# A Mamba-and-attention kernel on one core: output products of high and low parts, B's table re-read through DRAM, divisions one per tile

## The chip, the core and the metric

The kernel runs on one core of a Trainium2 chip. Its five engines are TensorE (PE; its weight loads are shown as PEld), VectorE (DVE), ScalarE (ACT), GpSimd (POOL) and SyncE (SP, which here only issues DMAs). The metric is device time in microseconds (us) of one execution, lower is better.

## The reference, cut to what matters

The reference is a block of a state-space layer (L0) and an attention layer (L1), both residual, on x of shape (4, 1024, 512). The change is in L0's scan and in L1's last projection. What L0 computes, cut:

```python
xr, gate = jnp.split(x @ W_in.T, 2, axis=-1)
xc = silu(conv(xr + t_emb))                      # 4 taps, per channel
xn = layernorm(xc) * ln_g + ln_b                 # (4, 1024, 1024)
Bm, Cm, dt = jnp.split(xn @ W_xproj.T, 3, axis=-1)
Ad = 1.0 + tanh(dt @ W_dt.T + b_dt) * 0.01 * A
def step(h, inputs):                             # 1024 steps, h is (4, 16, 1024)
    h = jnp.clip(h * ad[:, :, None] + bd[:, :, None] * xt[:, None, :], -10.0, 10.0)
    return h, jnp.einsum('bd,bdh->bh', ct, h)
y = ys + D * xn
x1 = x + (y * silu(gate)) @ W_out.T
```

L1 is attention with 16 heads; at its end the attended rows are divided by the softmax sums and multiplied with w_weight.

## The kernel before, in words

The kernel goes through a pre-phase (in-projection, convolution, norm; up to about 435 us), the scan (466 to 1422 us), a short phase in which the scan's last tiles are put out beside the first work of L1 (1427 to 1491 us), the projections of L1, the attention, and an out phase (2799 us to the end).

**The scan.** `scan_phase` has 32 iterations (`LOOPS`) of 32 steps, and each iteration has 16 pairs of steps (`PAIRS`). All four batches go through each step together. VectorE does the recurrence, one custom instruction of 128x512 a step (L905). Each engine has its own program, ordered by hand, and they meet on semaphores. In `pe_loop` TensorE's order for two pairs v and v+1 is: the outer products of B and x for pair v (`products_bx`, L1023, into the PSUM tile `bx`, one of two buffers); in some places a `turn`, four transposes of the gated rows `yg` into `p_turn`; two pieces from `ORDER`; the outer products for pair v+1; the readouts of pairs v-2 and v-1 (L1033). I call such two pairs a period. There are eight in an iteration, and `ORDER` gives them: gate, gate, out, out, gate, gate, out, out. A gate piece is three fp32r products of 128x128 by 128x512 (high by high, high by low, low by high; L940). An out piece is one of the eight products (m = 0 to 7) of the output projection of tile j, one plain fp32 matmul, which the profile shows as two instructions (L949). The turns stand in the periods v = 0 (a gate period) and v = 4 (an out period). For the first five iterations (`OUT_LAG`) there is no tile to put out, and each out piece is replaced by four fp32r products whose result nobody reads (L955).

**What stands around an out piece.** A tile of 128 rows is mixed by POOL (`mix`, L910, L913, L916: times D, plus the scan's y, times the gate, into `yg`), turned by TensorE, copied by ACT from `p_turn` to `yg_t` (`take_turned`, L973), multiplied, and copied out by ACT (`take_out`, L977). ACT takes the first half's turn right after the last four stores of the scan's y of the iteration before (L1079).

**B's table.** POOL writes `b_weights` and `c_weights` for each half (i = 0 and 1) of an iteration (L1007, L1009) as soon as the buffer is free, and TensorE waits for them at the first pair of that half. `b_weights` comes from `bd_all`, a table of B of 128 partitions by 16 KB. It is spread from DRAM by `load_bd`: twelve DMAs, whose source has a leading dimension of 4 or 2 copies with step 0. The part for the first four iterations is loaded ahead of the scan, under `consts_in`, for which VectorE waits before its last two set-up instructions; the rest is loaded inside the scan, under `bd_in`, for which POOL waits only ahead of iteration 4. SP issues the loads of x (`load_moving`, eight DMAs a half) as the buffers come free.

**After the scan** five tiles are still to be put out (`out_tile`); VectorE does their mixes, and POOL scales x1 for L1 (`scale_x1`, L195).

**The out phase.** For each of 32 tiles TensorE multiplies into one of four PSUM banks, and VectorE scales (L1831) and adds the residual (L1823). The last batch's four row blocks are first divided by the softmax sums on VectorE (`divide`, L1750), cast by ACT (L1809) and their low parts are taken by POOL (L1817). Tile 24 is the first that needs them.

Of the kernel before, what the change touches and what calls it, by code (L numbers as in the profile page):

```python
# [8 lines left out]
f32 = mybir.dt.float32  # L9
f32r = mybir.dt.float32r  # L10
# [4 lines left out]
P = 128  # L15
# [728 lines left out]
def scan_phase(nc, I, Xp, Xn, Bp, Pd, Iv, Cm, Y, SG, X1, pj, shared, used_before):  # L744
# [26 lines left out]
    with ExitStack() as ctx:  # L771
# [6 lines left out]
        w_out = sb("w_out", [P, NM, MODEL], f32); d_row = sb("d_row", [P, INNER], f32); ident = sb("ident", [P, P], f32)  # L778
        y = sb("y", [P, INNER], f32)
        w_plain = shared; xn, sg_in, yg = (shared[:, i, :] for i in range(3)); yg_t = shared[:, 3, :].rearrange("p (m t) -> p m t", t=P)  # L780
# [5 lines left out]
        bd_all = sb("bd_all", [P, SEQ // PHASES * STATES], f32)  # L786
# [17 lines left out]
        w_high = sem("w_high"); x_high = sem("x_high"); x_split = sem("x_split"); others_in = sem("others_in"); xn_in = sem("xn_in"); y_in = sem("y_in"); res_in = sem("res_in"); mixed = sem("mixed"); gated = sem("gated"); turned = sem("turned"); turned_taken = sem("turned_taken")  # L804
        out_ready = sem("out_ready"); out_taken = sem("out_taken"); x1_ready = sem("x1_ready"); x1_out = pj.x1_out
        consts_in = sem("consts_in"); bd_in = sem("bd_in"); zeros_ready = sem("zeros_ready")
# [10 lines left out]
        EARLY = LAG * (STEPS // PHASES) * STATES  # L817

        def load_bd(e, done, begin, end, phases):
            for phase in phases:  # L820
                for row, part, copies in ((0, 0, 4), (4, 1, 2), (6, 0, 2)):
                    src = Bp[part, :, phase].rearrange("(o b) t d -> o b (t d)", o=1)[:, :, begin:end].to_broadcast([copies, BATCH, end - begin])
                    e.dma_start(bd_all[phase * GROUP + row * BATCH:phase * GROUP + (row + copies) * BATCH, begin:end], src).then_inc(done, 16)
# [8 lines left out]
        with nc.Block() as block:  # L832
            @block.sync
            def _(sp):
# [7 lines left out]
                load_bd(sp, consts_in, 0, EARLY, range(2, PHASES))  # L842
# [3 lines left out]
            def _(act):  # L846
                load_moving(act, 0, 0)
                act.dma_start(x_tile[:], I["x_tiles"][0]).then_inc(tile_in, 16)
                load_bd(act, consts_in, 0, EARLY, range(2))
# [57 lines left out]
        def mix(e, engine, j):  # L907

            e.wait_ge(xn_in, START + j * 32 + 32)
            engine.tensor_tensor(out=xn, in0=xn, in1=d_row[:], op=ALU.mult).then_inc(mixed, 1)  # L910
# [20 lines left out]
        def piece_of(pe, it, j, piece):  # L931
# [66 lines left out]
        def pool_loop(pool, it, j, out=False, split=True):  # L998
            for i in range(2):
                if i == 1 and split:  # L1000
                    split_low(pool, it)
# [913 lines left out]
```

## Time and profile before

| | |
|---|---|
| time, median of 3 runs | 2910.11 us (2899.70 to 2910.88) |
| the profiled execution | 2906.17 us, span 2904.4 us |
| mean granted TensorE clock | 0.968 of 2.4 GHz |
| PE busy | 2739.1 us, 94% of the span |
| DVE busy | 2006.8 us, 69% |
| ACT, POOL busy | 1166.8 us and 1157.4 us, 40% each |
| HBM traffic | 258.88 MB read, 160.98 MB written |

The span runs from the first to the last instruction of the profiled execution, and its time is 1.8 us longer. Matmuls overlap in the records, so a busy PE is not one at its peak; the starts of instructions on the timeline are the better measure there.

### The profile page before, as it was taken

The numbers are of one execution on the slowest core, as the hardware profiler recorded it, in microseconds if no ns is written. First come the engines' busy times: TensorE is split into PE (matmuls) and PEld (weight loads), VectorE is DVE, ScalarE is ACT, GpSimd is POOL, SyncE is SP. The second block draws the span as 40 slices with busy tenths as digits, with TensorE's granted clock in tenths as the row PEclk, the third lists the DMA queues.
The fourth block names the chain that finished last, engine by engine and source line by source line (L and its number), as shares of the span: only waits on it lengthen the run. The fifth ranks groups of instructions, "written<-read, shape, count | busy, mean of one in ns | idle before, by whom it ended". The sixth has DMA issues, their size and how long they took to land. (4 is left out here: it accounts for less than half of the span.)

```text
span 2904.4 us, 53855 instructions
## 1 busy us (share of the span) xinstructions
PE 2739.1 (94%) x20345; PEld 1425.5 (49%) x20346; DVE 2006.8 (69%) x2121; ACT 1166.8 (40%) x1979; POOL 1157.4 (40%) x504
## 2 busy tenths in 40 slices
PE   7999955999999999999889999969999999999998
PEld 3444323665555555555457877833333333333337
DVE  2788867888888888888743333367777777777625
ACT  2677851211111111111222122126666666666640
POOL 0000001134445444444311212026667777777762
PEclk9999967999999999999999999979999999999999
DMA  3246475577777777777644344472244344343256
GB/s 106 87 156 218 179 245 112 131 155 172 170 161 169 168 170 166 169 166 172 175 131 163 131 148 155 149 194 66 67 111 109 95 125 107 99 124 111 83 189 209
DMA packets 246891, 421.92 MB, mean 145 GB/s; under 512 B 45848, under 2 KB 114072, under 8 KB 240360
## 3 DMA queue, kind: packets, MB, share of 16 engines
q1 hardware_dynamic: 164168, 330.57, 39.4%
q10 hardware_dynamic: 82592, 89.67, 13.7%
q8 instruction: 74, 1.21, 0.2%
q14 instruction: 57, 0.47, 0.1%
HBM read 258.88 MB, written 160.98 MB: 145 GB/s over the span
## 5 line engine op out<-in xcount | busy, mean ns | idle before, releaser
L905 DVE CUSTOM_DVE_ANT_0 b_h<-b_h,b_bx,b_bounds_all 128x512 f32<-128x512 f32 x1024 | 825.7, 806 | 134.5 <-PE b_bx L1023 95.1
L1576 DVE TENSOR_REDUCE e_half_max<-ef_banks 128x4 f32<-128x2048 f32 x256 | 586.3, 2293 | 235.0 <-PE ef_banks L1529 235.0
L1719 POOL TENSOR_TENSOR e_pair_sum<-e_probs 128x2048 f32<-128x2048 f32 x128 | 586.7, 4584 | 265.7 <-PE ef_banks L1568 214.2
L1688 ACT ACTIVATE e_probs<-ef_banks 128x512 f32<-128x512 f32 x1024 | 556.0, 595 | 311.3 <-PE ef_banks L1543 311.2
L1007 POOL TENSOR_TENSOR b_b_weights<-b_bd_all,b_mask_b 128x512 fp32r<-128x512 f32 x64 | 82.4, 1287 | 768.4 <-POOLq L832 462.4
L1543 PE MATMUL ef_banks<-e_qs,e_ks 97*128 97x512 f32 x1024 | 382.9, 453 | 3.9 <-DVE e_half_max L1576 3.6
L1074 ACT COPY b_y_stage<-b_y_psum 128x128 f32<-128x128 f32 x256 | 68.1, 266 | 648.8 <-PE b_y_psum L1033 648.6
L1543 PEld LDWEIGHTS ef_banks<-e_qs,e_ks 97*128 97x128 f32 x1024 | 155.0, 189 | 332.0 <-ACT e_probs L1688 311.8
L1023 PE MATMUL b_bx<-b_x_moving,b_b_weights 24*128 24x512 f32 x1024 | 256.6, 497 | 31.5 <-POOL b_c_weights L1009 29.7
L1033 PE MATMUL b_y_psum<-b_h,b_c_weights 128*32 128x128 f32 x8224 | 278.6, 276 | 0.5 <-ACT b_y_stage L1074 0.5
L1553 PE MATMUL ef_banks<-e_probs,e_v 128*32 128x512 f32 x2048 | 274.5, 608 | 0.5 <-ACT e_probs L1688 0.4
L949 PE MATMUL b_p_out<-b_w_out,shared 128*128 128x512 f32 x512 | 254.3, 623 | 7.9 <-ACT shared L973 7.9
L1033 PEld LDWEIGHTS b_y_psum<-b_h,b_c_weights 128*32 128x32 f32 x8224 | 209.4, 110 | 63.7 <-issue 62.8
L1023 PEld LDWEIGHTS b_bx<-b_x_moving,b_b_weights 24*128 24x128 f32 x1024 | 94.7, 182 | 219.0 <-DVE b_h L905 167.0
L531 DVE SCALAR_TENSOR_TENSOR a_acc<-a_padded,a_cols,a_acc 128x1024 f32<-128x1024 f32 x96 | 123.3, 1284 | 69.9 <-ACT a_acc L445 67.7
L1568 PE MATMUL ef_banks<-e_pair_sum,e_lanes 128*32 128x256 f32 (+1 forms) x2016 | 162.3, 394 | 3.3 <-POOL e_pair_sum L1719 2.7
L1529 PE MATMUL ef_banks<-ef_mats 32*128 32x512 f32 x1024 | 134.2, 511 | 20.5 <-DVE e_half_max L1576 15.0
L913 POOL TENSOR_TENSOR shared<-shared,b_y 128x1024 f32<-128x1024 f32 x28 | 66.7, 2382 | 210.1 <-DMA b_y<-scan_out 210.1
L949 PEld LDWEIGHTS b_p_out<-b_w_out,shared 128*128 128x128 f32 x512 | 89.8, 194 | 99.7 <-issue 89.3
L359 PE MATMUL a_p_rows<-a_x_t,a_w_in 128*128 128x512 f32 x256 | 116.1, 608 | 19.2 <-DMA a_w_in<-in_w_in_t_dram 18.9
L195 POOL TENSOR_TENSOR d_xl<-d_x,d_s_row 128x512 f32<-128x512 f32 x32 | 42.4, 1333 | 211.4 <-DMA d_x<-x_tiles 211.4
L359 PE MATMUL a_p_rows<-shared,a_w_in 128*128 128x512 f32 x256 | 115.5, 605 | 0.5 <-ACT a_xn L456 0.5
(217 smaller groups left out, 3724.1 us busy)
## 6 DMA issues: line engine op xcount, KB each, us to landing
b_x_moving<-xn_parts SPq DMA_DIRECT2D x252, 128.0 KB
e_ks<-qk_parts ACTq DMA_DIRECT2D x42, 512.0 KB, 4.8
e_qs<-qk_parts ACTq DMA_DIRECT2D x84, 256.0 KB, 3.5
xn_full<-a_xn SPq DMA_DIRECT2D x32, 512.0 KB, 3.2
xn_parts<-a_hi SPq DMA_DIRECT2D x64, 256.0 KB, 2.5
xn_parts<-a_lo SPq DMA_DIRECT2D x64, 256.0 KB, 2.5
silu_gate<-b_sg ACTq DMA_DIRECT2D x64, 256.0 KB, 6.6
scan_out<-b_y_stage ACTq DMA_DIRECT2D x256, 64.0 KB, 4.4
```

Of the source, the lines that this page charges most:

```text
L359: mm = nc.tensor.matmul(p_rows[m % 2][:, h * 512:h * 512 + 512], w_in[:, k, m * P:(m + 1) * P], x_t[n % 2][:, k, h * 512:h * 512 + 512], s ...
L905: return nc.vector._custom_dve(bass.dve_ops.TENSOR_ADD_SAT, **operands)
L949: mm = nc.tensor.matmul(p_out[:], yg_t[:, m, :], w_out[:, m, :], start=(m == 0), stop=(m == NM - 1))
L1023: m = nc.tensor.matmul(bx[v % 2][:, r, :], b_weights[e * GROUP:e * GROUP + K, i, k, :], x_moving[e * GROUP:e * GROUP + K, i, k, :], start= ...
L1033: m = nc.tensor.matmul(y_psum[32 * j:32 * j + 32, 0:128], c_weights[:, (u // T) % 2, u % T, :], h[:, u % RING, 128 * j:128 * j + 128], sta ...
L1529: mm = nc.tensor.matmul(to[:, h, :], qm[i][h * HD:(h + 1) * HD, rows], km[i][h * HD:(h + 1) * HD, keys * 512:(keys + 1) * 512], start=True ...
L1543: nc.tensor.matmul(p_exp[h % 2], ks[i][:, h, kt * P:(kt + 1) * P], qs[i][:, half, h, :], start=True, stop=True).then_inc(scores, 1)
L1553: mm = nc.tensor.matmul(p_o[HD * h:HD * (h + 1), :], v[n % RING][:, kt, HD * h:HD * (h + 1)], probs[:, g % 4, h, :], start=(kt == 0), stop ...
L1568: mm = nc.tensor.matmul(p_d[HD * h:HD * (h + 1), cols], lanes[:, lane, :], pair_sum[:, t % 2, h, cols], start=(within == 0), stop=(within ...
L1576: nc.vector.tensor_reduce(out=half_max[:, u // UNITS % 2, :, r // NH, r % NH], in_=(banks[:, u % 2 * GROUP:(u % 2 + 1) * GROUP] if u < FIR ...
L1688: nc.scalar.activation(probs[:, g % 4, h, :], p_exp[h % 2], ACT.Exp).then_inc(exps, 1)
L1719: nc.gpsimd.tensor_tensor(out=pair_sum[:, t % 2], in0=probs[:, (2 * t) % 4], in1=probs[:, (2 * t + 1) % 4], op=ALU.add).then_inc(paired, 1)
```

## The change

Three parts, and what they bring with them.

1. Each out piece becomes three fp32r products (high by high, high by low, low by high) instead of one fp32 product. `w_out` is split in the third iteration (it = 2): ACT casts four blocks of 128x1024, POOL takes the low parts. `take_turned` becomes two copies on ACT (`yg_t` and `yg_hi`), and POOL takes the low part (`low_turned`), once ahead of the second half's weights and once ahead of `mix`. The second turn waits for both copies of the first, and the out pieces wait for `low_ready`. The unread products go from four to three a piece. `d_row` moves into `shared` and is loaded later. After the scan both turns stand ahead of a tile's pieces, and POOL takes the low parts between its `scale_x1`.
2. `bd_all` goes. Ahead of the scan only the first iteration's part of B is loaded. In the scan's block SP issues the same twelve spreading DMAs, now from DRAM to a DRAM table `Bx`, waits until they have landed, and only then goes on to the loads of iteration 1. Each half then has one DMA of 128 x 256 B ahead of its eight loads of x, and POOL waits for it.
3. The last batch's divisions stand at tiles 16, 17, 18 and 19 instead of 17, 19, 21 and 23.

```diff
+        def spread_b(e, dst, done, end, phases):
             for phase in phases:
                 for row, part, copies in ((0, 0, 4), (4, 1, 2), (6, 0, 2)):
+                    src = Bp[part, :, phase].rearrange("(o b) t d -> o b (t d)", o=1)[:, :, 0:end].to_broadcast([copies, BATCH, end])
+                    e.dma_start(dst[phase * GROUP + row * BATCH:phase * GROUP + (row + copies) * BATCH, 0:end], src).then_inc(done, 16)
+        def load_bd(e, it, i):
+            e.dma_start(bd[:, i, :], Bx[:, bass.ds((it * (STEPS // PHASES) + i * (T // PHASES)) * STATES, T // PHASES * STATES)]).then_inc(bd_in[i], 16)
-                load_bd(sp, consts_in, 0, EARLY, range(2, PHASES))
+                spread_b(sp, first_bd, consts_in, STEPS // PHASES * STATES, range(2, PHASES))
...
-            pe.wait_ge(turned_taken, START + j * 2 + g)
+            pe.wait_ge(turned_taken, START + j * 4 + 2 * g)
...
-                    pe.wait_ge(turned_taken, START + j * 2 + m // 4 + 1)
+                    pe.wait_ge(low_ready, START + j * 2 + m // 4 + 1)
-                mm = nc.tensor.matmul(p_out[:], yg_t[:, m, :], w_out[:, m, :], start=(m == 0), stop=(m == NM - 1))
+                for part, (rows, weights) in enumerate(((yg_hi, w_out_hi), (yg_hi, w_out_lo), (yg_lo, w_out_hi))):
+                    mm = nc.tensor.matmul(p_out[:], rows[:, m, :], weights[:, m, :], start=(m == 0 and part == 0), stop=(m == NM - 1 and part == 2))
...
-                for part in (w_hi, w_hi, w_lo, w_lo):
+                for part in (w_hi, w_lo, w_hi):
...
-            nc.scalar.copy(yg_t[:, 4 * g:4 * g + 4, :], p_turn[:].rearrange("p (m t) -> p m t", m=4)).then_inc(turned_taken, 1)
+            nc.scalar.copy(yg_t[:, g], p_turn[:].rearrange("p (m t) -> p m t", m=4)).then_inc(turned_taken, 1)
+            nc.scalar.copy(yg_hi[:, 4 * g:4 * g + 4, :], p_turn[:].rearrange("p (m t) -> p m t", m=4)).then_inc(turned_taken, 1)
+        def low_turned(pool, j, g):
+            pool.wait_ge(turned_taken, START + j * 4 + 2 * g + 2)
+            nc.gpsimd.tensor_tensor(out=yg_lo[:, 4 * g:4 * g + 4, :], in0=yg_t[:, g], in1=yg_hi[:, 4 * g:4 * g + 4, :].bitcast(f32), op=ALU.subtract).then_inc(low_ready, 1)
...
                 sp.wait_ge(read, START + it * PAIRS + (10 + 8 * i))
+                load_bd(sp, it, i)
                 load_moving(sp, it, i)
...
                 if i == 1 and split:
                     split_low(pool, it)
+                if i == 1 and low:
+                    low_turned(pool, j + (-1), 0)
                 pool.wait_ge(read, START + it * PAIRS + (10 + 8 * i))
+                pool.wait_ge(bd_in[i], START + it * 16)
...
             if out:
                 add_x(pool, nc.gpsimd, j + (-2))
+            if low:
+                low_turned(pool, j + (-1), 1)
             if j is not None:
                 mix(pool, nc.gpsimd, j)
...
                 load_tile(sp, 1)
-                load_bd(sp, bd_in, EARLY, SEQ // PHASES * STATES, range(PHASES))
+                spread_b(sp, Bx, spread, SEQ // PHASES * STATES, range(PHASES))
+                sp.wait_ge(spread, START + 3 * PHASES * 16)
                 sp_loop(sp, 1, None)
...
             for g in range(2):
                 turn(pe, j, g)
-                for piece in OUT[g * (NM // 2):(g + 1) * (NM // 2)]:
-                    piece_of(pe, None, j, piece)
+            for piece in OUT:
+                piece_of(pe, None, j, piece)
...
-                    if t % 2 == 1 and t // NQ == BATCH - 2:
-                        divide(dve, BATCH - 1, t % NQ // 2)
+                    if t // NQ == BATCH - 2 and t % NQ < NK:
+                        divide(dve, BATCH - 1, t % NQ)
```

## Rows read from the trace of the kernel before

**Rows 1.** Costliest groups: the recurrence; busy us, mean ns, idle before it and releaser.

```profile
L905 DVE CUSTOM_DVE_ANT_0 b_h<-b_h,b_bx,b_bounds_all 128x512 f32<-128x512 f32 x1024 | 825.7, 806 | 134.5 <-PE b_bx L1023 95.1
```

**Rows 2.** Windows: stretch and length, busy us of each engine, PEclk, DMA share, GB/s.

```profile
826.00:946.00 120.00, 120.00 (x1374) 69.22 (x1366) 104.26 (x130) 21.91 (x58) 56.59 (x36) 1.00 0.73 168
```

**Rows 3.** Timeline, a gate period, then an out period: start, us, engine, line, operation.

```profile
904.86 0.50 PE L1023 MATMUL b_bx<-b_x_moving,b_b_weights 24*128 24x512 f32 x2
...
908.31 0.50 PE L1023 MATMUL b_bx<-b_x_moving,b_b_weights 24*128 24x512 f32 x2
...
911.29 3.34 DVE L905 CUSTOM_DVE_ANT_0 b_h<-b_h,b_bx,b_bounds_all 128x512 f32<-128x512 f32 x4 [0.45 <-PE b_bx L1023]
912.10 0.50 PE L1023 MATMUL b_bx<-b_x_moving,b_b_weights 24*128 24x512 f32 x2
```

**Rows 4.** Timeline, from the period ahead to the end of the out period with a turn.

```profile
919.72 0.50 PE L1023 MATMUL b_bx<-b_x_moving,b_b_weights 24*128 24x512 f32 x2
...
922.58 0.59 ACT L973 COPY shared<-b_p_turn 128x512 f32<-128x512 f32 x1 [2.46 <-issue]
...
923.58 0.42 PEld L928 LDWEIGHTS b_p_turn<-b_ident,shared 128*128 128x128 f32 x4 [0.24 <-issue]
...
923.97 0.30 PEld L949 LDWEIGHTS b_p_out<-b_w_out,shared 128*128 128x128 f32 x2
...
925.89 0.50 PE L1023 MATMUL b_bx<-b_x_moving,b_b_weights 24*128 24x512 f32 x2
...
927.33 0.51 PE L1023 MATMUL b_bx<-b_x_moving,b_b_weights 24*128 24x512 f32 x2
```

**Rows 5.** Groups by line: POOL's subtraction of the same shape as `low_turned`.

```profile
L969 POOL TENSOR_TENSOR b_x_lo<-b_x_tile,b_x_hi 128x512 fp32r<-128x512 f32 x31 | 39.8, 1285 | 14.2 <-ACT b_x_hi L966 14.0
```

**Rows 6.** Timeline, POOL waiting for the scan's y in `mix`.

```profile
903.08 2.38 POOL L913 TENSOR_TENSOR shared<-shared,b_y 128x1024 f32<-128x1024 f32 x1 [6.84 <-DMA b_y<-scan_out]
```

**Rows 7.** Timeline, first and last product of a period with unread products.

```profile
555.83 0.50 PE L1023 MATMUL b_bx<-b_x_moving,b_b_weights 24*128 24x512 f32 x2
...
559.74 0.50 PE L1023 MATMUL b_bx<-b_x_moving,b_b_weights 24*128 24x512 f32 x2
```

**Rows 8.** Timeline, the scan's start: VectorE's wait, SP's DMAs, iteration 1's first product.

```profile
460.07 0.69 DVE L871 TENSOR_SCALAR b_bounds_all<-b_bounds_all 128x1024 f32<-128x1024 f32 x1 [3.12 <-DMA b_bd_all<-b_parts]
...
462.57 7.81 SPq L823 DMA_DIRECT2D b_bd_all<-b_parts  x12
...
487.91 3.96 SPq L830 DMA_DIRECT2D b_x_moving<-xn_parts  x8
...
499.03 0.50 PE L1023 MATMUL b_bx<-b_x_moving,b_b_weights 24*128 24x512 f32 x2
```

**Rows 9.** Windows of 2 us while the spreading DMAs run (columns as in rows 2).

```profile
468.00:470.00 2.00, 2.00 (x13) 0.89 (x15) 0.21 (x1) 0.00 (x0) 0.00 (x0) 0.50 0.25 108
...
484.00:486.00 2.00, 2.00 (x23) 1.36 (x15) 1.93 (x3) 0.27 (x1) 0.00 (x0) 1.00 0.14 58
```

**Rows 10.** DMA issues from 440 to 500 us: KB each, median us to landing.

```profile
b_x_tile<-in_x_tiles_dram SPq DMA_DIRECT2D x1, 256.0 KB, 2.5
```

**Rows 11.** Timeline behind the scan: out pieces after a long and after a short wait.

```profile
1428.72 6.45 PE L949 MATMUL b_p_out<-b_w_out,shared 128*128 128x512 f32 x8 [0.68 <-ACT shared L973]
...
1453.05 3.70 PE L949 MATMUL b_p_out<-b_w_out,shared 128*128 128x512 f32 x8 [0.68 <-ACT shared L973]
```

**Rows 12.** Timeline of the out phase: a division, a low part, an addition, TensorE's wait.

```profile
2857.57 1.22 DVE L1750 TENSOR_TENSOR f_ot<-f_ot,f_rd 128x1024 f32<-128x1024 f32 x1
...
2860.01 2.39 POOL L1817 TENSOR_TENSOR f_ot_lo<-f_ot,f_ot_hi 128x1024 fp32r<-128x1024 f32 x1 [20.89 <-ACT f_ot_hi L1809]
...
2860.50 2.45 DVE L1823 TENSOR_TENSOR f_o<-f_x,f_o 128x512 f32<-128x512 f32 x1
...
2878.29 0.79 PE L1797 MATMUL ef_banks<-f_w_hi,f_ot_hi 128*128 128x512 f32 x1 [3.99 <-POOL f_ot_lo L1817]
```

**Rows 13.** The chain that ended last: its last stretch of products, start, us, what.

```profile
2878.29 21.54 PE ef_banks L1797 x87
```

More of the change, by code:

```diff
@@ L777, in sem @@
             return sems[-1]
[L778 removed]
+        w_out_hi = sb("w_out_hi", [P, NM, MODEL], f32r); w_out_lo = sb("w_out_lo", [P, NM, MODEL], f32r); ident = pj.ident
         y = sb("y", [P, INNER], f32)
[L780 removed]
+        w_plain = shared; xn, sg_in, yg, d_row = (shared[:, i, :] for i in range(4)); w_out_plain = shared[:].rearrange("p k (a n) -> p (k a) n", n=MODEL)
+        yg_t = sb("yg_t", [P, 2, NM // 2, P], f32); yg_hi = sb("yg_hi", [P, NM, P], f32r); yg_lo = sb("yg_lo", [P, NM, P], f32r)
         x = sb("x", [P, MODEL], f32); o = sb("o", [P, MODEL], f32); x1 = sb("x1", [P, MODEL], f32)
@@ L909, in mix @@
             e.wait_ge(xn_in, START + j * 32 + 32)
-            engine.tensor_tensor(out=xn, in0=xn, in1=d_row[:], op=ALU.mult).then_inc(mixed, 1)
+            engine.tensor_tensor(out=xn, in0=xn, in1=d_row, op=ALU.mult).then_inc(mixed, 1)
             e.wait_ge(mixed, START + j * 2 + 1)
@@ L995, in sp_loop, with pool_loop @@
                     load_x(sp, j + (-1), *before)
-        def pool_loop(pool, it, j, out=False, split=True):
+        def pool_loop(pool, it, j, out=False, split=True, low=False):
             for i in range(2):
@@ L1082, in act_loop @@
                     take_gate(act, it, 0)
+                if split_out and q < 4:
+                    out_high_part(act, q)
                 if q == 4:
@@ L1112, in _ @@
                 pool_loop(pool, 0, None, split=False)
-                with pool.Fori(1, LAG) as it:
-                    pool_loop(pool, it, None)
-                pool.wait_ge(bd_in, START + 3 * PHASES * 16)
-                pool.wait_ge(others_in, START + 48)
+                pool_loop(pool, 1, None)
+                pool_loop(pool, 2, None)
+                for c in range(4):
+                    out_low_part(pool, c)
+                pool_loop(pool, 3, None)
+                pool.wait_ge(d_in, START + 16)
                 pool_loop(pool, LAG, 0)
-                pool_loop(pool, LAG + 1, 1)
+                pool_loop(pool, LAG + 1, 1, low=True)
                 with pool.Fori(2, TILES - LAG) as j:
-                    pool_loop(pool, j + LAG, j, True)
+                    pool_loop(pool, j + LAG, j, True, low=True)
             @block.tensor
@@ L1124, in _ @@
                     pe_loop(pe, it, None)
[L1125 removed]
+                pe.wait_ge(out_split, START + 4)
                 with pe.Fori(0, TILES - OUT_LAG) as j:
@@ L1179, in _ @@
             def _(pool):
-                for q in range(NQ):
-                    pj.scale_x1(pool, 0, q, True)
+                for n, j in enumerate(range(first - 1, last + 1)):
+                    for g in range(2):
+                        low_turned(pool, j, g)
+                    for q in range(2 * n, min(2 * n + 2, NQ - 1)):
+                        pj.scale_x1(pool, 0, q, True)
+                    if j == last - 1:
+                        pj.scale_x1(pool, 0, NQ - 1, True)
             @block.tensor
```

43 lines of the change are left out of this document (24 added, 19 removed).

## The prediction

> **What bounds the kernel now.** I read the groups by line first, to find what the scan's recurrence waits for. VectorE spends 825.7 us in 1024 steps of 806 ns, and sits idle 134.5 us ahead of them, 95.1 us of it for TensorE's outer products [rows 1]. The scan (466 to 1422 us) is thus VectorE's steps plus what TensorE makes them wait. The windows say that TensorE's clock is granted in full there, 1.00 or 2.4 GHz, and that DMA is at 0.76 [rows 2]. Then I read one iteration on the timeline and measured each period from one product L1023 to the same one of the next period. A gate period takes 908.31 - 904.86 = 3.45 us, and an out period 912.10 - 908.31 = 3.79, with VectorE idle 0.45 in it [rows 3]. Four steps of 806 ns are 3.22, and their gaps bring them close to 3.45, so I take 3.45 as the floor of a period. The out period with a turn ends at 927.33 [rows 4]; from the product at 923.16 (919.72 plus a gate period, and 0.42 ahead of the turn's 923.58), that is 4.17. An iteration takes some 29.7 us.
>
> **Out pieces.** Two out pieces cost 925.89 - 923.97 = 1.92 us from their first weight load to the next product [rows 4]. As triples they cost what a gate's two pieces cost: 1.92 less the difference of the periods (3.79 - 3.45 = 0.34) [rows 3], so 1.58. Three of the four out periods of an iteration gain 0.34 each, 1.0 us an iteration.
>
> **The wait that this adds.** The fourth out period, v = 4, has the second turn and the pieces m = 0 to 3 directly behind it. ACT reaches the first copy at 922.58 only, since it stands behind the four stores' issue [rows 4]. A copy takes 0.59, so the second ends 1.1 to 1.2 us after that start, at 923.7. POOL then needs 1.285 us for the low part [rows 5] and some 0.1 for each handover: 925.1 to 925.2. TensorE's turn moves from 923.58 to about 923.75 and is over before that, so the triples start at 925.15 where the fp32 pieces started at 923.97 [rows 4]. With 1.58 for them the next product comes at 926.7 instead of 925.89, +0.85. Behind the waiting TensorE are that product, and so VectorE's next steps; nothing later in the iteration gives it back, since the other periods are at their floor. Bounds: 0.75 (the copies overlap a little and a handover takes 0.05) to 1.0. An iteration comes to -1.0 + 0.85 = -0.15, and 27 iterations have a tile: -4 us, between -7 and 0.
>
> **The rest of POOL and ACT in an iteration.** POOL's second half's weights now end about 7.7 us after 919.72, and their first user comes at 931.1. The second low part ends before 10.5, the first mix product before 12.8. The sum with y is not later than before, because it waits for y's load anyway: it starts at 903.08 after 6.84 us idle [rows 6], which is 13.1 after its iteration's like of 919.72. Cost nothing; if y landed earlier or POOL were 0.4 us slower, mix would slip, but its user, the turn, has 8 us more. SP issues one more DMA ahead of each eight loads of x, 0.4 us; these land 5 us and more ahead of their use.
>
> **Unread products.** A period with eight of them takes 559.74 - 555.83 = 3.91 us [rows 7]; with six it is a gate period, 3.45. That is 0.46, four times in an iteration: -7.4 us for iterations 1 to 4. Iteration 0's 1.8 us are in the next part.
>
> **The scan's start.** VectorE waits 3.12 us for B's table [rows 8]. A quarter of the bytes is loaded there now, so I take the whole wait away: -3.1 (bound 0). Then the spreading DMAs. They held a DMA share of 0.25 at 108 GB/s and later 0.14 at 58 [rows 9]: 4 of the 16 engines, then about 2, each at some 26 GB/s. By the code, the DMAs with 4 copies sit on four engines and those with 2 copies on two of these. With 16 KB a row, the two busiest get 4 x 3 x 4 rows = 768 KB each: 29.7 us at 26.5 GB/s. From the first issue [rows 8] it takes 2.4 us to the first packet and 1 to 2 for the last landing, so SP goes on 33.5 us after it. Before, SP did not wait and issued x's loads 487.91 - 462.57 = 25.3 after it [rows 8]. Now the DMA for B and eight loads follow: 0.4 + 3.96 of issue [rows 8] and up to 2.5 to land [rows 10], so iteration 1 starts 39.9 us after the first issue. It started 499.03 - 462.57 = 36.5 after it [rows 8]: +3.4, and TensorE, 1.8 earlier by the shorter products, stands idle for 5 us. Such waits cost the clock here: after one of over 4 us (between the scan's end at 1422 and the next phase's start at 1427) eight out instructions took 6.45 us instead of 3.70 [rows 11], 2.75 more, while 0.68 us of waiting did nothing. I take +2.5. Together -3.1 + 3.4 + 2.5 = +2.8.
>
> The Trainium skill (DMA: Bandwidth & Descriptors, Why a DMA increments its semaphore by 16 and not by 1) says that the slowest dimension of both access patterns sets on how many engines a DMA runs, so that a leading broadcast of 4 or 2 copies confines it to as many. By that rule, the trace agrees for the loads into SBUF, and a DRAM target changes nothing: the sum above stands. Without the rule, a DRAM-to-DRAM copy could use all sixteen, which is the second rival below.
>
> **w_out's split** is four casts on ACT and four subtractions on POOL in iteration 2. POOL's take some 2.4 us each, as in the out phase [rows 12], and end about 18 us into an iteration whose next weights are due at 26. Nothing; if they slipped by over 4 us, iteration 3 would start late.
>
> **Behind the scan** the chain there goes through loads and VectorE's mixes, and a tile's pieces are not on it. POOL now puts eight low parts of 1.285 us [rows 5] and two to four scalings into stretches where VectorE worked alone, and an addition beside POOL takes 2.45 us where the usual one takes 0.7 [rows 12]. Some 5 us of POOL's work meet the chain, and POOL's scalings no longer meet an earlier stretch. I take +2, bounds -1 and +6.
>
> **Out phase.** TensorE waits 3.99 us for the last low part [rows 12], and its last 87 products take 21.54 us [rows 13], which is 0.248 each and 3.0 a tile of twelve. At best the 3.99 go, and what the wait costs in clock besides, up to the 2.75 of [rows 11]: 6.7. Against it: a division, 1.22, a blocked addition, 2.45 with POOL's 2.39 [rows 12], and now at every tile. In the worst order a tile costs VectorE 1.2 + 0.6 + 0.6 + 2.4 = 4.8 us against TensorE's 3.0, the fourth low part ends near 2875.5 instead of 2878.2, and 2.7 are gained. The first division may also wait for its blocks, which would have to be there by 2855 where they were used at 2857.6. I take -3.5, nearer to the lower end.
>
> **Sum.** -4 - 7.4 + 2.8 + 2 - 3.5 = -10 us. Against the profiled execution, 2906.2, that gives 2896; against the median of the runs shown, 2910.1, it gives 2900. I take 2898. No change can be told from one below 0.5%, 14.5 us.
>
> **Rivals.**
> 1. The forecast, chance 0.50, own range 2888 to 2908. For it speak the chain ACT, POOL, TensorE at v = 4, whose steps all have a row, and the engine share of the spreading.
> 2. The copy to DRAM is quick and SP never late. Then +3.4 and +2.5 go, and iteration 0's -1.8 counts: -18, 2890. Against it: the DMA share [rows 9]. Chance 0.15.
> 3. The wait at v = 4 doesn't come, because ACT gets to its copies sooner or the pieces find the low part ready: 27 x 0.85 = 23 less, 2875. Against it is ACT's place in its order [rows 4]. Chance 0.08.
> 4. Slower: a DRAM-to-DRAM row takes twice as long as a DRAM-to-SBUF one, so that SP is held for 63 us instead of 33.5: +30, 2928. No row shows such a copy. It decides from about 10 us over my 29.7 on. Chance 0.12.
> 5. Slower: TensorE loses its clock at each v = 4, 27 x 2.5 = 68, 2965. Against it: the wait there is about 1 us, and waits of 0.68 leave eight instructions at 3.70 [rows 11]. Chance 0.05.
>
> 0.10 is left for what lies between, in the stretch behind the scan above all.
>
> **Numbers.** Faster by over 0.5%: nearly all of rival 2 (0.13) and 3 (0.08), 0.12 of the forecast, 0.03 of the rest: 0.36. Slower: rivals 4 and 5 and 0.02: 0.19. Between: 0.45. The range takes in rivals 2 and 3 and the milder half of rival 4: 2874 to 2924.
>
> **What would show it.** In the profile after: seven periods of 3.45 to 3.85 in an iteration and one of 5.0 at v = 4, with TensorE's first out weights waiting for POOL's `yg_lo`; iterations of 29.6; those of the first five 27.6; SP's first loads of x some 33.5 us after the first spreading DMA, and a granted clock of 0.5 just behind; VectorE's wait ahead of L871 gone; TensorE's wait in the out phase at most 3 us. The prediction is wrong if v = 4 takes 4 us or 6, if the spreading is done within 25 us or lasts over 40, or if the stretch behind the scan grows by over 6.

## The result and the profile after

The changed kernel takes 2919.61 us, median of 15 runs (2915.53 to 2923.30), and the kernel before, run beside it, 2908.11 us (15 runs, 2899.70 to 2913.49). The ratio is 1.0040, 95% interval 1.0031 to 1.0049: 11.5 us slower, where some 10 us faster were forecast (2898 us). The profiled execution has a span of 2917.4 us against 2904.4, +13.0.

I cut both traces at the same places: VectorE's steps are as long as before and their idle time grew, in the page's groups by line [rows 1]:

```profile
L909 DVE CUSTOM_DVE_ANT_0 b_h<-b_h,b_bx,b_bounds_all 128x512 f32<-128x512 f32 x1024 | 825.7, 806 | 148.8 <-PE b_bx L1043 98.8
```

| stretch | before | after | difference | forecast |
|---|---|---|---|---|
| first outer product at | 465.28 | 462.05 | -3.2 | -3.1 |
| iterations 0 to 4 | 153.3 | 155.9 | +2.6 | -1.5 |
| iteration 5 to the last outer product | 801.2 | 812.9 | +11.7 | -4 |
| from there to VectorE's last shift of the first norm | 60.3 | 68.6 | +8.3 | +2 |
| projections and attention, to the out phase | 1318.9 | 1318.3 | -0.5 | 0 |
| out phase | 105.4 | 99.6 | -5.8 | -3.5 |

The sum of the differences is +13.1.

**An iteration.** The timeline of the same iteration as in [rows 4] (here it starts at 918.67, before at 915.87), from its second period on:

```profile
922.50 0.50 PE L1043 MATMUL b_bx<-b_x_moving,b_b_weights 24*128 24x512 f32 x2
922.78 0.33 SPq L827 DMA_DIRECT2D b_bd<-b_spread  x1
923.08 2.27 ACTq L1099 DMA_DIRECT2D scan_out<-b_y_stage  x4
...
925.77 0.59 ACT L978 COPY b_yg_t<-b_p_turn 128x512 f32<-128x512 f32 x1 [2.87 <-issue]
925.95 0.18 PEld L1043 LDWEIGHTS b_bx<-b_x_moving,b_b_weights 24*128 24x128 f32 x2 [0.20 <-DVE b_h L909]
...
926.26 0.59 ACT L979 CAST b_yg_hi<-b_p_turn 128x512 fp32r<-128x512 f32 x1
...
926.90 0.66 PE L932 MATMUL b_p_turn<-d_ident,shared 128*128 128x128 f32 x4 [0.45 <-ACT b_yg_hi L979]
926.92 1.27 POOL L982 TENSOR_TENSOR b_yg_lo<-b_yg_t,b_yg_hi 128x512 fp32r<-128x512 f32 x1 [11.64 <-ACT b_yg_hi L979]
...
929.91 0.49 PE L1043 MATMUL b_bx<-b_x_moving,b_b_weights 24*128 24x512 f32 x2
...
938.54 0.34 SPq L827 DMA_DIRECT2D b_bd<-b_spread  x1
...
939.07 3.36 SPq L834 DMA_DIRECT2D b_x_moving<-xn_parts  x8
...
949.22 0.49 PE L1043 MATMUL b_bx<-b_x_moving,b_b_weights 24*128 24x512 f32 x2 [0.54 <-DMA b_x_moving<-xn_parts]
```

The wait at v = 4 is there as forecast: ACT's two copies behind the stores, POOL's low part, then the products. In this iteration ACT's four stores took 2.27 us to issue and the period v = 4 took 5.39; in most iterations it is some 1.9 and 5.0. The last row is what was not forecast. TensorE stands at the first product of the next iteration and waits for x: the issue of its last load ended at 942.43, and the product starts 6.8 us later. The view of one line (L1043, 560 to 1420 us) sums these waits up:

```profile
its engine sat idle before it (us, times) until:
  DVE b_h L909: 133.8, 423
  DMA b_x_moving<-xn_parts: 13.3, 22
```

The same view of the kernel before (L1023, 610 to 1420 us) names no DMA. I measured the eight periods of every iteration by the starts of their first products. The means over iterations 6 to 30 are, in order of v:

| | v=0 | 2 | 4 | 6 | 8 | 10 | 12 | 14 | iteration |
|---|---|---|---|---|---|---|---|---|---|
| before | 3.85 | 3.44 | 4.18 | 3.79 | 3.46 | 3.45 | 3.79 | 3.77 | 29.73 |
| after | 3.85 | 3.46 | 5.03 | 3.45 | 3.45 | 3.45 | 3.45 | 4.08 | 30.22 |

Seven of the eight periods are the forecast's. The eighth should have been 3.45 and is 4.08.

**The start.** Timeline from the set-up to iteration 1 [rows 8]:

```profile
456.80 0.69 DVE L875 TENSOR_SCALAR b_bounds_all<-b_bounds_all 128x1024 f32<-128x1024 f32 x1 [0.79 <-DMA b_bd<-b_parts]
...
459.31 7.94 SPq L822 DMA_DIRECT2D b_spread<-b_parts  x12
...
492.70 0.35 SPq L827 DMA_DIRECT2D b_bd<-b_spread  x1
493.10 2.95 SPq L834 DMA_DIRECT2D b_x_moving<-xn_parts  x8
...
502.21 0.79 PE L1043 MATMUL b_bx<-b_x_moving,b_b_weights 24*128 24x512 f32 x2 [10.51 <-DMA b_x_moving<-xn_parts]
```

SP goes on 33.4 us behind its first spreading DMA, where 33.5 were forecast. The product comes at 42.9 behind it and not at 39.9: it starts 6.2 us after the last issue of x's loads. TensorE was idle for 10.5 us, the windows show a granted clock of 0.50 (1.2 GHz) there, and the first period behind it takes 5.85 us instead of 3.45.

**Behind the scan**, VectorE's splits and a mix beside POOL:

```profile
1456.58 2.28 DVE L167 TENSOR_TENSOR d_w_q_lo<-d_w_q,d_w_q_hi 128x2048 fp32r<-128x2048 f32 x1
...
1457.02 6.25 POOL L982 TENSOR_TENSOR b_yg_lo<-b_yg_t,b_yg_hi 128x512 fp32r<-128x512 f32 x2 [8.81 <-ACT b_yg_hi L979]
...
1458.78 3.35 DVE L167 TENSOR_TENSOR d_w_k_lo<-d_w_k,d_w_k_hi 128x2048 fp32r<-128x2048 f32 x1
...
1462.06 3.36 DVE L167 TENSOR_TENSOR d_w_v_lo<-d_w_v,d_w_v_hi 128x2048 fp32r<-128x2048 f32 x1
1463.24 5.54 POOL L195 TENSOR_TENSOR d_xl<-d_x,d_s_row 128x512 f32<-128x512 f32 x2
1465.35 2.31 DVE L914 TENSOR_TENSOR shared<-shared 128x1024 f32<-128x1024 f32 x1
```

**The out phase** in the chain that ended last [rows 12, 13]:

```profile
2817.80 29.75 PE ef_banks L1822 x64
2847.54 65.34 PE ef_banks L1830 x288
```

The wait of 3.99 us is gone; all 288 products run in one piece.

### The profile page after: what moved, and what is told of

Same layout as the page of the kernel before. It is cut to its first block and busy times, and to the rows that moved or that the text cites. A ratio compares the mean times of both kernels' runs of the same rounds, so it can differ in the third digit from the quotient of the medians.

```text
span 2917.4 us, 54601 instructions
## 1 busy us (share of the span) xinstructions
PE 2700.9 (93%) x20561; PEld 1470.9 (50%) x20562; DVE 2012.0 (69%) x2121; ACT 1191.2 (41%) x2041; POOL 1258.6 (43%) x572
## 5 line engine op out<-in xcount | busy, mean ns | idle before, releaser
L1094 ACT COPY b_y_stage<-b_y_psum 128x128 f32<-128x128 f32 x256 | 68.6, 268 | 652.5 <-PE b_y_psum L1053 651.2
L1576 PEld LDWEIGHTS ef_banks<-e_qs,e_ks 97*128 97x128 f32 x1024 | 155.0, 189 | 332.1 <-ACT e_probs L1721 311.9
L1025 POOL TENSOR_TENSOR b_b_weights<-b_bd,b_mask_b 128x512 fp32r<-128x512 f32 x64 | 82.6, 1290 | 552.7 <-POOLq L836 459.2
L1043 PE MATMUL b_bx<-b_x_moving,b_b_weights 24*128 24x512 f32 x1024 | 256.3, 496 | 54.6 <-POOL b_c_weights L1027 27.4
L982 POOL TENSOR_TENSOR b_yg_lo<-b_yg_t,b_yg_hi 128x512 fp32r<-128x512 f32 x64 | 86.4, 1351 | 356.3 <-ACT b_yg_hi L979 356.3
L1043 PEld LDWEIGHTS b_bx<-b_x_moving,b_b_weights 24*128 24x128 f32 x1024 | 95.0, 182 | 200.9 <-DVE b_h L909 146.2
L954 PE MATMUL b_p_out<-b_w_out_hi,b_yg_hi 128*128 128x512 f32 x256 | 116.1, 454 | 24.4 <-POOL b_yg_lo L982 24.4
L944 PE MATMUL b_gate<-b_w_hi,b_x_hi 128*128 128x512 f32 x256 | 114.8, 448 | 0.0
```

Source lines behind the costliest of these rows:

```text
L1043: m = nc.tensor.matmul(bx[v % 2][:, r, :], b_weights[e * GROUP:e * GROUP + K, i, k, :], x_moving[e * GROUP:e * GROUP + K, i, k, :], start= ...
L1576: nc.tensor.matmul(p_exp[h % 2], ks[i][:, h, kt * P:(kt + 1) * P], qs[i][:, half, h, :], start=True, stop=True).then_inc(scores, 1)
```

## The experiments

Each ratio is to the kernel before, run on the same chip in the same rounds; the medians of the kernel before in these rounds lie between 2906.27 and 2910.13, so differences between two changed kernels are better taken from the ratios. "Its 0-4" and "iteration" (mean of iterations 6 to 30) are measured on the trace as above, "behind" from the last outer product to the first norm.

| kernel | median us | ratio (95%) | its 0-4 | iteration | behind |
|---|---|---|---|---|---|
| before | 2908.11 | 1 | 153.3 | 29.73 | 60.3 |
| after | 2919.61 | 1.0040 (1.0031 to 1.0049) | 155.9 | 30.22 | 68.6 |
| e1 short parts | 2899.62 | 0.9975 (0.9964 to 0.9986) | 153.7 | 29.73 | |
| e2 B's table | 2914.29 | 1.0027 (1.0016 to 1.0039) | 162.7 | 29.78 | |
| e3 B's load early | 2903.26 | 0.9992 (0.9981 to 1.0002) | 161.5 | 29.63 | 67.5 |
| e4 turn taken early | 2883.17 | 0.9924 (0.9907 to 0.9940) | 156.0 | 28.88 | 67.2 |
| e5 x triggered early | 2902.97 | 0.9984 (0.9974 to 0.9993) | 155.0 | 29.61 | 66.7 |
| e6 spread over 16 | 2919.70 | 1.0046 (1.0030 to 1.0063) | 145.4 | 30.60 | 68.4 |
| e7 low parts cut | 2914.23 | 1.0027 (1.0018 to 1.0037) | 156.0 | 30.21 | 63.9 |
| e8 three mended | 2854.33 | 0.9815 (0.9799 to 0.9831) | 142.3 | 28.40 | 67.0 |
| e9 e8, old tail order | 2859.79 | 0.9830 (0.9807 to 0.9852) | 140.5 | 28.40 | 70.1 |
| e10 e6 and e3 | 2892.35 | 0.9938 (0.9917 to 0.9959) | 144.7 | 29.72 | 66.9 |
| e11 e8, scalings first | 2852.11 | 0.9807 (0.9794 to 0.9821) | 140.3 | 28.42 | 64.7 |
| e12 before, x early | 2910.14 | 0.9999 (0.9986 to 1.0013) | 155.2 | 29.76 | 60.6 |

### e1: the unread products and the divisions alone

```diff
-                for part in (w_hi, w_hi, w_lo, w_lo):
+                for part in (w_hi, w_lo, w_hi):
-                    if t % 2 == 1 and t // NQ == BATCH - 2:
-                        divide(dve, BATCH - 1, t % NQ // 2)
+                    if t // NQ == BATCH - 2 and t % NQ < NK:
+                        divide(dve, BATCH - 1, t % NQ)
```

> The kernel before with two parts alone: six unread products a period instead of eight, and the last batch's divisions at tiles 16 to 19. Theory (both are independent of the rest): the unread periods fall from 3.91 to 3.45, which gives 5.5 to 7.4 us in iterations 1 to 4 and nothing in iteration 0, whose end waits for x; the out phase, with TensorE's last 87 products no longer behind a wait of 3.99 us, gives 5 to 6.7. Together -12 us, between -10 and -14. Rival (the out phase gained in the changed kernel from something else, such as its earlier clock): only the unread part is left, -5 to -8.

Measured: -7.3 by the ratio, where -12 was expected. The number lies in the rival's range of -5 to -8, but the trace shows the opposite of the rival: the out phase takes 99.2 us instead of 105.4, so the divisions are worth 6 us by themselves, and the shorter unread products are worth nothing here. Iterations 3 and 4 fall to 27.6, and iterations 0 to 2 grow by as much. TensorE only reaches the wait for x sooner, and then runs slower: its products of B and x take 0.8 us instead of 0.5, and the periods behind the two waits 5.20 and 5.71 us instead of 3.45. (The profiled execution was the slowest of the eight, 2903.49; its projections and attention took 3.3 us more than before, which the edit does not touch. The others could differ at the start too.)

```profile
501.19 0.80 PE L1023 MATMUL b_bx<-b_x_moving,b_b_weights 24*128 24x512 f32 x2 [5.51 <-DMA b_x_moving<-xn_parts]
...
534.17 0.79 PE L1023 MATMUL b_bx<-b_x_moving,b_b_weights 24*128 24x512 f32 x2 [3.55 <-DMA b_x_moving<-xn_parts]
```

### e2: B's table alone

The kernel before with `spread_b`, `Bx` and this, out pieces and unread products as before:

```diff
+                sp.wait_ge(spread, START + 3 * PHASES * 16)
...
+                load_bd(sp, it, i)
                 load_moving(sp, it, i)
```

> The kernel before with B's table through DRAM alone: spreading DMAs to DRAM with SP waiting for them, one DMA for B ahead of each eight loads of x. Theory (x's chain: the iteration's first product waits for eight loads that SP issues 19.3 us into the iteration before and that land 6.8 us after the last issue): with 0.53 us more in front, the landing comes at 19.3 + 10.7 = 29.9 against an iteration of 29.73, so iterations of 29.9, +0.2 each, +5 over 27 (0 to +6); the start costs iteration 0 some +6 (40.2 instead of 33.8), less 3.2 for VectorE's wait, and +2 to +3 for the clock behind it. Together +11 us, between +6 and +15. Rival (x's loads have room and the longer last period of the changed kernel comes from its out pieces or from POOL): iterations of 29.73, and +6 us in all.

Measured +7.9, with iterations of 29.78, which is nearer to the rival's +6 and 29.73 than to the theory's +11 and 29.9. Nearly all is at the start, 9.3 us in iterations 0 to 4 less 3.5 for the first product; the loop grows by 0.05 an iteration. My 0.2 came from an offset of 19.3 us for SP's trigger, which is 19.0 by the trace (934.87 less 915.87). With that, x lands at 19.0 + 10.7 = 29.7, just in time for 29.73. By that sum the DMA for B is harmless in the loop as long as nothing else is taken from the time between trigger and use. This run alone does not show that x's chain is what counts; e3 and e5 do.

### e3 and e5: what stands ahead of x's loads

e3 issues only B's DMA at the earlier event, e5 both:

```diff
e3:
+                sp.wait_ge(bx_ready, START + it * PAIRS + (8 * i - 8))
                 load_bd(sp, it, i)
+                sp.wait_ge(read, START + it * PAIRS + (10 + 8 * i))
                 load_moving(sp, it, i)
e5:
-                sp.wait_ge(read, START + it * PAIRS + (10 + 8 * i))
+                sp.wait_ge(bx_ready, START + it * PAIRS + (8 * i - 8))
                 load_bd(sp, it, i)
                 load_moving(sp, it, i)
```

> The changed kernel, where SP issues the DMA for B as soon as the half's last outer product is done, some 4 us before it may issue x's loads, so that it no longer stands between the trigger and these. Theory (x's chain sets the iteration's end): the last period falls from 4.08 to 3.55 us, iterations from 30.22 to 29.7, 26 times 0.5 = -13 us against the changed kernel, so 2906 or a ratio to the kernel before of 0.9995. Rival (POOL's low parts delay the weights): no change, 2919, ratio 1.004.

> The changed kernel, where SP issues both B's DMA and the eight loads of x when the half's last outer product is done, and not a period later, when its readouts are done too. Theory (x lands too late at the iteration's end by some 0.6 us): the last period is 3.45 us instead of 4.08, iterations 29.6, -17 us over 27, and 1 to 2 more in iterations 1 to 3: 2901, ratio 0.9975. VectorE's wait at v = 4 stays at 5.03. Rival (the DMA engines are full, so that loads issued earlier only take longer, and those of the gated tile behind them come later and hold POOL): under -8 us, 2912 or more.

Both theories hold. In e3 the last period falls to 3.55 and the iteration to 29.63; in e5 they are 3.45 and 29.61. The period at v = 4 stays at 4.98 and 5.05. The view of one line (620 to 1420 us) of e3:

```profile
  DMA b_x_moving<-xn_parts: 1.9, 5
```

and of e5 there is no such row. POOL's low parts are as they were, so they did not hold the weights. In the profiled execution of e3 iterations 0 to 4 take 5.6 us more than in the changed kernel: iteration 1 ends in a wait (its last period takes 6.23 us), and iteration 2, 32.05 us long, starts at the lower clock. The median lies below that execution's 2909, so others seem to pay less; why is open.

### e4: ACT takes the first turned half ahead of the stores

```diff
-                if q == 0 and j is not None:
-                    take_turned(act, j, 0)
...
                 if q == 7 and j is not None:
                     take_out(act, j)
+                if q == 7 and following is not None:
+                    take_turned(act, following, 0)
                 act.wait_ge(read, START + it * PAIRS + (BEFORE + 2 * q + 4))
```

(The calls that hand over `following` are left out here.)

> The changed kernel, where ACT takes the first turned half before it waits for the last readout of the iteration before, so ahead of the four stores of the scan's y. Theory (the wait at v = 4 is ACT's place in its order, and x's chain sets the iteration's end): the period at v = 4 falls from 5.03 to 3.83 us, SP's trigger comes 1.2 us earlier, x lands at 18.7 + 10.7 = 29.35 in the iteration, so iterations of 29.35 instead of 30.22: 27 times 0.87 = -23 us, 2896, ratio 0.996. Rival 1 (x's chain is not what sets the last period): the whole 1.2 is gained, -32 us, 2887. Rival 2 (POOL is the limit at v = 4, not ACT): under -8 us.

The period at v = 4 falls from 5.03 to 3.85, so the wait there was ACT's place in its order. The iteration falls by 1.34 and the time by 34 us against the changed kernel. That is rival 1's number, but it does not speak for rival 1. I had made the theory's 29.35 from the trigger of one iteration whose v = 4 took 5.39 us. In the mean iteration the trigger is at 15.79 + 3.74 = 19.5 us (four periods, and 3.74 from v = 8 to SP's issue), and 19.5 + 10.7 = 30.2, which is the iteration measured. With 1.18 less, the same sum gives 29.0, and 28.88 was measured. The period v = 4 lies ahead of the trigger, so a shorter one is gained whole under either theory, and this run could not tell them apart. e3 and e5 do. What is left of x's wait shows in the last period, 3.93.

### e6 and e10: the spreading over 16 engines

```diff
+                for row, part, copies in ((0, 0, 4), (4, 1, 2), (6, 0, 2)):
+                    src = Bp[part].rearrange("b p (o t) d -> (b p) o (t d)", o=1).to_broadcast([BATCH * PHASES, copies, SEQ // PHASES * STATES])
+                    sp.dma_start(Bx[:].rearrange("(g c) n -> g c n", c=8)[:, row:row + copies, :], src).then_inc(spread, 16)
+                sp.wait_ge(spread, START + 3 * 16)
```

These lines take the place of the twelve spreading DMAs and of SP's wait for them; `load_bd` changes too, to read the rows of `Bx` in the new order (left out here).

> The changed kernel, where B is spread to DRAM by three DMAs whose outermost dimension has 16 rows (batch by phase) in both patterns, with the copies behind it, and each half's DMA for B reads the rows in that order. Theory (the twelve DMAs ran on 4 and then 2 of the 16 engines): 2 MB on 16 engines take some 8 us with issue and landing, so SP waits for nothing but its trigger, iteration 0 takes 31 us instead of 40.2 and loses at most little of the clock behind it: -9 to -11.5 us, 2909, ratio 1.0005. Rival (such a copy is bounded by DRAM or by its own packets and not by the number of engines): SP still goes on 25 us or more behind the first issue, at most -3 us.

Windows of e6 (columns as in rows 2): the spreading is over at 467, 8 us behind its first issue at 458.95.

```profile
462.00:464.00 2.00, 2.00 (x6) 1.31 (x5) 1.34 (x2) 0.00 (x0) 0.00 (x0) 0.50 0.95 360
464.00:466.00 2.00, 2.00 (x9) 0.81 (x8) 0.28 (x1) 0.00 (x0) 0.00 (x0) 0.50 0.93 385
466.00:468.00 2.00, 2.00 (x38) 1.48 (x37) 1.73 (x3) 0.00 (x0) 0.63 (x1) 0.90 0.25 107
```

The start gains 10.5 us, as the theory says. The Trainium skill (DMA: Bandwidth & Descriptors, Why a DMA increments its semaphore by 16 and not by 1) lets a DMA use as many engines, up to 16, as divide the slowest dimension of both patterns; the run agrees, with 33.4 us for a leading 4 or 2 and 8 for a leading 16.

The whole time did not move, since the loop gave the 10 us back: 30.60 an iteration. The DMA for B now gathers rows in another order, and its issue takes 0.56 us instead of 0.34, ahead of x's loads and beside ACT's four stores. In e6:

```profile
944.98 0.56 SPq L827 DMA_DIRECT2D b_bd<-b_spread  x1
945.27 2.27 ACTq L1099 DMA_DIRECT2D scan_out<-b_y_stage  x4
945.72 3.47 SPq L834 DMA_DIRECT2D b_x_moving<-xn_parts  x8
```

The same place in a usual iteration of the changed kernel:

```profile
893.15 0.33 SPq L827 DMA_DIRECT2D b_bd<-b_spread  x1
893.44 1.92 ACTq L1099 DMA_DIRECT2D scan_out<-b_y_stage  x4
893.66 3.38 SPq L834 DMA_DIRECT2D b_x_moving<-xn_parts  x8
```

By the means over iterations 6 to 30, x's wait is the smaller share of the 10 us. The last period grew by 0.12 (4.08 to 4.20), 3 us in 26 iterations. The period at v = 4 grew by 0.21 (5.03 to 5.24), 5.5 us: the issue of ACT's four stores takes 2.12 us on average and not 1.92, up to 2.27, and ACT's copies stand behind it. The length of v = 4 follows the length of this issue in each iteration, in both kernels. Once, behind iteration 26, TensorE waited 1.63 us for x and the next period took 5.33 us instead of 3.85 (granted clock 0.82 from 1280 to 1286), 1.5 us more.

e10 is e6 with e3's edit.

> The changed kernel with the spreading over 16 rows and, besides, B's DMA issued when the half's last outer product is done, as in the second batch's first edit of SP; x's loads keep their trigger. Theory (the run with the spreading alone gained 10.5 us in iterations 0 to 4 and gave them back because its DMA for B takes 0.56 instead of 0.34 us to issue ahead of x's loads): the iterations fall from 30.6 to 29.65, and the start's gain stays: 27 times 0.57 = -15 and -10 to -12 us against the changed kernel: 2893, ratio 0.9955. Rival (the longer iterations come from the new pattern's packets on the DMA engines and not from its place in SP's order): iterations of 30.0 and more, 2903.

e10 came out as its theory says: 2892.35 for 2893, 29.72 for 29.65. The last period is 3.63, and v = 4 is back at 4.99 with 1.88 us for ACT's stores. So the DMA costs what it costs because of its place in SP's order, but in two ways: ahead of x's loads, and beside ACT's stores. That its packets slowed x is not seen: by the updates of x's semaphore in the traces, the last load landed 6.5 us after its issue in e6 and 6.7 in the changed kernel and in e10 (means of 25 iterations).

### e7, e9 and e11: the stretch behind the scan

e7 narrows POOL's ten low parts there to 32 columns; e9 is e8 with the old order of turns and products; e11 is e8 with POOL's seven scalings in a row:

```diff
e7:
-                        low_turned(pool, j, g)
+                        pool.wait_ge(turned_taken, START + j * 4 + 2 * g + 2)
+                        nc.gpsimd.tensor_tensor(out=yg_lo[:, 4 * g, 0:32], in0=yg_t[:, g, 0, 0:32], in1=yg_hi[:, 4 * g, 0:32].bitcast(f32), op=ALU.subtract).then_inc(low_ready, 1)
e9:
-            for piece in OUT:
-                piece_of(pe, None, j, piece)
+                for piece in OUT[g * (NM // 2):(g + 1) * (NM // 2)]:
+                    piece_of(pe, None, j, piece)
e11:
-                    for q in range(2 * n, min(2 * n + 2, NQ - 1)):
+                    for q in range(NQ - 1) if n == 0 else ():
```

> The changed kernel, where POOL's ten subtractions behind the scan take 128x32 instead of 128x512 (most of the low parts of the last five tiles are left out); all waits stay. Theory (behind the scan VectorE's splits and mixes run beside POOL and are slowed by it, 3.36 instead of 2.28 us and 2.2 instead of 1.23): VectorE's chain is 3 to 8 us shorter, -5 us, 2914.5. Rival (the stretch is longer because of ACT's second copy and of both turns standing ahead of the products): at most -2 us.

> The run with the three mended waits (2854), where behind the scan each tile's first turned half is multiplied before the second is turned, as in the kernel before. What is open: the stretch from the last outer product to the first norm (VectorE's last shift before ACT's root) is 68.6 us in the changed kernel, 60.3 before, and 63.9 with the low parts cut, so 3.6 are not POOL's. Theory (both turns ahead of the products let the last half's low part come early, and the 3.6 are the second copy of each half and the later load of y): the old order is no better, 0 to +3 us, 2854 to 2857. Rival (the 3.6 come from the new order): -2 to -3.6 us, 2851.

> The run with the three mended waits (2854), where POOL behind the scan does its first seven scalings of x1 in a row behind the first tile's low parts, instead of two behind each tile's. What is open: 3.6 of the 8.3 us by which the stretch behind the scan grew are neither the low parts nor the order of the turns. Theory (they are the scalings, which now run beside VectorE's mixes of the last three tiles and take them from 1.23 to 2.2 us each): these mixes are free again, some five of them by 1.0, against two of the first mix that are slowed as they were in the kernel before: -3 us (-1 to -4), 2851, ratio 0.9805, and the stretch from the last outer product to the first norm is 63 to 64 us instead of 67.0. Rival (the mixes are not on the chain there, which goes through loads): within 1 us, 2854.

Of the 8.3 us, 4.7 are the low parts (68.6 to 63.9; 3.8 in the time, by the ratios). The new order of the turns is not a cost: the old one is 3.1 us longer behind the scan, and 4.4 in the time by the ratios, whose intervals overlap, where 0 to 3 was expected. The scalings' new places are 2.3 us (67.0 to 64.7); in the time this is 2.2 and the two intervals overlap, so the trace alone carries it. Each of these figures is from one profiled execution, and the stretch differs between kernels whose code is the same there: after, e3, e4, e5, e6, e8 and e10 take 66.7 to 68.6. e7 and e11 lie 2.8 and 2.0 us below the lowest of them and e9 1.5 above the highest, so the signs are safe and the sizes are not, by up to 2 us. In e11 the mix that took 2.31, 2.17 and 1.23 us in the changed kernel runs free again:

```profile
1383.88 9.65 POOL L195 TENSOR_TENSOR d_xl<-d_x,d_s_row 128x512 f32<-128x512 f32 x7
...
1403.90 1.21 DVE L914 TENSOR_TENSOR shared<-shared 128x1024 f32<-128x1024 f32 x1
1405.15 1.23 DVE L917 TENSOR_TENSOR shared<-shared,b_y 128x1024 f32<-128x1024 f32 x1
1406.41 1.23 DVE L920 TENSOR_TENSOR shared<-shared 128x1024 f32<-128x1024 f32 x1
```

Some 1.3 us of the 8.3 stay without a cause of their own, which is less than that spread.

### e8: the three mended together

e4, e5 and e6 in one kernel.

> The changed kernel with three edits at once: ACT takes the first turned half ahead of the stores, SP issues B's and x's loads when the half's last outer product is done, and the spreading to DRAM is three DMAs over 16 rows. Theory (the edits undo three separate waits): against the run with ACT's edit alone, 2883, the iterations fall from 28.88 to 28.4 (periods 3.85, 3.45, 3.85 and five of 3.45), -13 us, and the start by 9 to 11.5: 2859, ratio 0.983. Rival (x's landing is bounded by the DMA engines' load, which grows as iterations get shorter): iterations of 28.9, 2872.

Measured 2854.33, with every steady iteration at 28.40: the two periods with a turn take 3.85, the other six 3.45. No product of this kernel waits for a DMA from iteration 1 on. With e11's edit it is 2852.11, ratio 0.9807, 1.9% below the kernel before. So the change does hold a gain, which the order of three engines' work around it hid.

### e12: the kernel before with x's loads early

```diff
-                sp.wait_ge(read, START + it * PAIRS + (10 + 8 * i))
+                sp.wait_ge(bx_ready, START + it * PAIRS + (8 * i - 8))
                 load_moving(sp, it, i)
```

> The kernel before, where SP issues the eight loads of x when the half's last outer product is done instead of when its readouts are. Theory (in the kernel before x's loads still landed in time, 29.6 against iterations of 29.73, by some 0.1 to 0.3 us): the steady iterations stay at 29.73, and only iterations 0 and 1, whose ends wait for x (5.76 instead of 3.90 in the last period of iteration 1), gain 1 to 3 us: 2905, ratio 0.999. Rival (loads of x issued earlier push the loads and stores behind them and hold POOL or ACT): +3 us or more.

Measured no change, 29.76 an iteration. The kernel before was not held by x in its loop. The gain that I expected at the start did not come either.

## Why the prediction was wrong

**The step that failed** is "SP issues one more DMA ahead of each eight loads of x, 0.4 us; these land 5 us and more ahead of their use". I had read the landing of one 256 KB load [rows 10] and not that of eight under the loop's traffic. There the first product that waits for them starts 6.8 us after the last issue (7.0 on average over the 23 iterations that end in such a wait, 6.4 to 7.7). What counts is the time from SP's trigger, 3.75 us into the period v = 8, to x's use at the iteration's end:

| | from trigger to use | issue and landing of x | left |
|---|---|---|---|
| before | 14.47 - 3.75 = 10.72 | 3.36 + 6.79 = 10.1 | +0.6 |
| e2, with B's DMA | 10.72 | 10.1 + 0.53 = 10.7 | 0.0 |
| after, shorter out periods too | 4 x 3.45 - 3.75 = 10.05 | 10.7 | -0.6 |
| e3, shorter out periods alone | 10.05 | 10.1 | -0.1 |

The four rows give the last period of each kernel: 3.77, 3.83, 4.08 and 3.55. The row of the kernel before takes its 6.79 from the changed kernel, since nothing waits for x there. The updates of x's semaphore in the two traces bear it out: on average over 25 iterations the last load lands 6.7 us after its issue in both kernels, which is 0.8 us ahead of its use before (0.4 to 1.3) and 0.2 after, where 0.2 is the handover. So the room was 0.6 us and not 5. B's DMA spent 0.53 of it and the two shorter out periods behind the trigger 0.67. Each alone was nearly free (e2, e3), and with both there and SP's trigger earlier the last period is 3.45 (e5); the second is the very gain of the triples. Together they cost 0.63 an iteration, +16 us, which is all that the loop missed by.

**Out pieces and the wait at v = 4**: right. Out periods fell by 0.34 each and v = 4 took 5.03 for 5.0. The 0.85 of the wait was right, and nothing gave it back. e4 shows that it needn't have been there: ACT had time for the first copy before its stores.

**The start**: the 33.5 us, the clock's +2.4 and VectorE's -3.2 were right; the landing of x was 6.2 us and not 2.5, the same mistake as in the loop, and worth 3.7; the issue of the loads was 1.0 shorter than taken, and the prediction's own terms add up to 40.4 and not 39.9, so 3.0 of it showed. "Unread products, -7.4" holds only if nothing else ends the iteration. e1 shows that in the kernel before they would have brought nothing. In the changed kernel, which differs from e2 there mostly by them, iterations 0 to 4 are 6.8 us shorter; but e3, with the same six products, took 161.5 there in its profiled execution, 1.2 less than e2, so what they are worth beside a late x stays open.

**Behind the scan**: the mechanism was right, POOL's work beside VectorE's, and the size was off: +8.3 for +2, outside my bound of 6. I counted some 5 us of overlap once, and eight low parts where ten run. Each POOL instruction there both takes longer and holds VectorE's. "POOL's scalings no longer meet an earlier stretch" missed what they meet instead, the mixes (e11, some 2.3 us). The Trainium skill (SBUF — State Buffer, SBUF: two separate sides) calls the port pair that VectorE and GpSimd share an exclusive lock: when a VectorE instruction has two inputs in SBUF and the GpSimd one reads SBUF, the one that starts second waits for the whole of the other. The trace fits it: two low parts of 1.28 us took 6.25 together beside two splits that took 3.35 and 3.36 instead of 2.28, which is not far from one of each in turn (1.28 + 2.28 = 3.56).

**The out phase**: -5.8 for -3.5, within the bound of 6.7. Besides the 3.99 us of the wait, the mean granted clock of the phase rose from 0.95 to 0.98. The divisions' worst order did occur (an addition of 2.30 us and a division of 3.42 beside two low parts of 6.19 together) and still ended in time.

**The rivals**: the copy did not take double, TensorE's clock was not lost at v = 4, the wait there came. None of the five held an x that lands too late. (In [rows 2] the DMA share is 0.73, not the 0.76 of the text; no term rests on it.) The three misses are +16 us in the loop, +6 behind the scan and +4 in iterations 0 to 4, against 2 gained more in the out phase.

## What to carry to other kernels

- For every load in a loop, write down trigger, issue, landing and use before an edit, with the landing read under that loop's own traffic. An issue put ahead of the load and work made shorter between trigger and use spend the same room, and they add up: a gain behind the trigger can be the one that runs into the load.
- Removing work that nobody reads gained nothing where a DMA ended the wait behind it, and the longer wait was paid in clock (e1).
- An issue on one engine can lengthen another engine's issues beside it: in e6, 0.22 us more on SP made ACT's stores 0.2 us longer on average, and that cost more than the delay of x.
- When a gain does not show, look for the next wait that ends last. Here three edits of order, each of a few lines, turned +0.4% into -1.85%.

## What the runs showed of the hardware

- While 2 MB were copied from DRAM to DRAM with a leading 16, the windows show 360 to 385 GB/s at a DMA share of 0.93 to 0.95 (e6, 8 us in all); the form with a leading 4 or 2 took four times as long, 33.4 us.
- A DMA of 128 rows of 256 B cost 0.34 us of SP's time in row order and 0.56 gathered as 32 by 4 rows. Beside the second form ACT took 2.12 us to issue four stores instead of 1.92 (e6).
- Eight loads of x were usable 6.2 us after their last issue even at the start, where the DMA share fell from 1.00 to 0.37 in the 2 us windows behind it, and some 7 us in the loop at a share of 0.74. The time from issue to use was thus nearly the same with the engines partly idle. Why, the runs don't settle.
